# Adaptive-norm Mamba block on one core: decay subtraction and clamp move from VectorE to ScalarE, the convolution goes in pairs of tiles

## The chip, the cores and the metric

The kernel runs on one core of a Trainium2 chip. The metric is the device time of one launch in microseconds; three runs of the kernel before were timed. A profile shows one further look at the same program, instruction by instruction. The engines are TensorE (PE for its matmuls, PEld for its weight loads), VectorE (DVE), ScalarE (ACT), GpSimd (POOL) and SyncE (SP), which issues DMAs.

## The reference, cut to what matters

Two sequences of 2048 tokens and 512 channels go through a norm with shift and scale, a state-space mixer with a gated residual, and then a norm, a feed-forward part with a gated residual. The change touches only the mixer:

```python
zxbcdt = u @ W_in.T                                     # 512 -> 1024 z, 1280 xBC, 16 dt
dt = jax.nn.softplus(dt_raw + dt_bias)                  # 16 heads
xBC = jax.nn.silu(causal_conv(xBC, W_conv, 4 taps) + b_conv)
x, Bm, Cm = split(xBC)                                  # 1024, 128, 128
# per chunk, with cs the running sum of dt*A and decay[l, s] = exp(cs[l] - cs[s]) for s <= l:
Y = ((C B^T) * decay) @ X + (C @ state) * exp(cs)
state = exp(cs_last) * state + B^T (X * exp(cs_last - cs))
y = (Y + Dp * X) * silu(z)
out = (y * rsqrt(mean(y*y) + 1e-5) * norm_w) @ W_out.T
```

## The kernel before, in words

The mixer works in 16 turns of 256 tokens (SC), each of NC = 2 chunks of 128. A turn n projects its own tokens, and does the decay and state work of the turn before it (u = n - 1) beside that; so a 17th turn has only the second half. Turns 0 to 2 and the last are unrolled, the others run in a loop whose body is two turns. There is no scheduler: the order on each engine is written out by hand in the `turn` functions (L572 GpSimd, L709 ScalarE, L983 VectorE, L1210 TensorE, L472 SyncE), and semaphores that count steps tie the engines together. An engine runs strictly in this order, so a wait holds up all behind it.

Around the change, in turn n:

- TensorE (L1210): scores_G, y_off(0,0), project_zdt(0), transpose_x(0), project_zdt(1), transpose_B(0), y_off(0,1), tile 0, y_diag(0,0), tile 1, y_diag(0,1), tiles 2 and 3, states(0,0), tile 4, states(0,1), transpose_x(1), tile 5, transpose_B(1), y_off(1,0), tile 6, cumulate, y_diag(1,0), transpose_g(0), tiles 7 and 8, project_out(0), y_off(1,1), y_diag(1,1), tile 9, z parts 0 and 1 with states(1,0) behind the first and states(1,1) behind the second, transpose_g(1), z parts 2 and 3, transpose_ln for turn n + 1, project_out(1). The pairs in brackets are (chunk, half of the heads).
- The projections alternate between two PSUM banks (`A_ORDER`, L375). A projection waits until the last but one before it has been read out (`a_emptied`): project_zdt(1) of turn n + 1 takes the bank of project_out(1) of turn n, and so waits for ScalarE's scale_out(1) (L702).
- ScalarE (L709) reads out each of the 10 tiles twice (L615, a copy for the convolution's taps; L616, its last tap with the bias), and at the end of the turn does evac_ln (L589), widen (L602), the SiLU of tiles 8 and 9 (L619), exp_sums (L678), four exp_decay (L686) of 128x1024 each, and scale_out(1). SiLU and Exp need a table load each, two in a turn.
- VectorE (L983): conv (L813) adds three taps to a tile, each instruction waiting for the one before it on the same tile. softplus (L843) is a chain of 15 instructions on 128x32. sums (L869) reads cumulate's products from PSUM. diff (L882), 32 instructions of 128x128 in a turn, makes min(cs[l] - cs[s], 0) in place in `A.L`, which a DMA has filled with cs[l] in every partition. read_state (L951) adds a state product from PSUM to the state; states(c,1) on TensorE uses the same PSUM bank and waits until read_state(c,0) is done. y_off(1,0) waits for read_state(0,1).
- GpSimd (L572) multiplies X by D (L535), and gates y in three instructions (L543, L547, L549) once VectorE has read y_diag and y_off of the chunk.
- SyncE (L472) writes the sums out (L484) and loads them back over all partitions (L493).

Of the kernel before, what the change touches and what calls it, by code (L numbers as in the profile page):

```python
# [8 lines left out]
ALU = mybir.AluOpType  # L9
ACT = mybir.ActivationFunctionType  # L10
# [28 lines left out]
def wait(eng, sem, n, per, c):  # L39

    v = count(n, per, c)
    if isinstance(v, int) and v <= 0:
        return
    eng.wait_ge(sem, v)
# [278 lines left out]
def mixer_stage(nc, T, A):  # L323
# [4 lines left out]
    D, DI, H, HD = T.D, T.DI, T.H, T.HD  # L328
    KD, KI = D // P, DI // P
    KH = KI // 2  # L330
    MX = T.CD // P
# [10 lines left out]
    with ExitStack() as ctx:  # L342
# [11 lines left out]
            sem(s) for s in ("silu_done", "siluq_done", "e3_done", "edt_done", "decay_done", "sq_done"))  # L354
        stats_step, normed, split, conv_step, softplus_step, sums_step = (
            sem(s) for s in ("stats_step", "normed", "split", "conv_step", "softplus_step", "sums_step"))
        tail_step, diff_done, G_masked, M_done, Xdec_done = (
            sem(s) for s in ("tail_step", "diff_done", "G_masked", "M_done", "Xdec_done"))
        yoff_read, ydiag_read, S_step = sem("yoff_read"), sem("ydiag_read"), sem("S_step")
        rstd_step, XD_done, y_summed, gated, rs_step, out_step = (  # L360
            sem(s) for s in ("rstd_step", "XD_done", "y_summed", "gated", "rs_step", "out_step"))
# [226 lines left out]
        def _(act):  # L588
# [29 lines left out]

            def silu_tile(n, b, m):  # L619

                wait(act, conv_step, n, 3 * MX, 3 * (m + 1))
                x = A.xc[b][:, m, :]
                nc.scalar.activation(x, x, ACT.Silu).then_inc(silu_done, 1)

# [53 lines left out]
            def exp_sums(u):  # L678
# [4 lines left out]
                wait(act, yoff_read, u, 2 * NC, 0)  # L683
                nc.scalar.activation(A.e3[:], A.s3[:], ACT.Exp).then_inc(e3_done, 1)

            def exp_decay(u, c, f):  # L686
                wait(act, diff_done, u, 2 * NC, 2 * c + f + 1)
                x = A.L[c][:, f * HH:(f + 1) * HH, :]
                nc.scalar.activation(x, x, ACT.Exp).then_inc(decay_done, 1)

            def exp_dt(n):
                wait(act, softplus_step, n, SP_STEPS, 2)
# [16 lines left out]
            def turn(n, b):  # L709
# [57 lines left out]
                if nxt:  # L767
                    evac_ln(after(n), 1 - b, n)
                if own:
                    widen(n, 1)  # L770
                    silu_tile(n, b, 8)
                    silu_tile(n, b, 9)
                    exp_sums(n)
                    exp_decay(n, 0, 0)
                    exp_decay(n, 0, 1)
                    exp_decay(n, 1, 0)
                    exp_decay(n, 1, 1)
# [6 lines left out]
        def _(dve):  # L784
# [25 lines left out]
                nc.vector.tensor_tensor(A.hTlo[:, :, s], h, A.hThi[:, :, s].bitcast(F32),  # L810
                                        ALU.subtract).then_inc(split, 1)

            def conv(n, b, m):  # L813

                a_wait(dve, a_emptied, n, ("m", m), 1)
                for j in range(3):
                    if j:
                        wait(dve, conv_step, n, 3 * MX, 3 * m + j)
                    nc.vector.scalar_tensor_tensor(A.xc[b][:, m, :], A.raw[:, m, j:j + SC], A.wconv[:, m, j:j + 1],  # L819
                                                   A.xc[b][:, m, :], ALU.mult, ALU.add).then_inc(conv_step, 1)  # L820

            def tails(n, b):

# [19 lines left out]
            def softplus(n):  # L843


                wait(dve, edt_done, n, 1, 1)
                step = [2]

                def did(ins):
                    ins.then_inc(softplus_step, 1)  # L850
                    step[0] += 1

                    wait(dve, softplus_step, n, SP_STEPS, step[0])

                did(nc.vector.tensor_scalar(sp2[:], sp1[:], 2.0, None, ALU.add))
                did(nc.vector.reciprocal(sp2[:], sp2[:]))
                did(nc.vector.tensor_tensor(sp3[:], sp1[:], sp2[:], ALU.mult))
                did(nc.vector.tensor_tensor(sp4[:], sp3[:], sp3[:], ALU.mult))
                did(nc.vector.tensor_scalar(sp5[:], sp4[:], 1.0 / 15.0, None, ALU.mult))
                for k in (13, 11, 9, 7, 5, 3):  # L860
                    did(nc.vector.scalar_tensor_tensor(sp5[:], sp5[:], 1.0 / k, sp4[:], ALU.add, ALU.mult))
                did(nc.vector.scalar_tensor_tensor(sp5[:], sp5[:], 1.0, sp3[:], ALU.add, ALU.mult))
                did(nc.vector.tensor_scalar(sp0[:], sp0[:], 0.0, None, ALU.max))
                did(nc.vector.scalar_tensor_tensor(sp5[:], sp5[:], 2.0, sp0[:], ALU.mult, ALU.add))

                nc.vector.tensor_tensor(A.a[:], sp5[:], A.negA[:].unsqueeze(1).broadcast_to([P, NC, H]),
                                        ALU.mult).then_inc(softplus_step, 1)

            def sums(n):  # L869

                wait(dve, cs_done, n, 1, 1)

                wait(dve, e3_done, n, 1, 0)
                wait(dve, cs_out, n, 16, 0)
                wait(dve, diff_done, n, 2 * NC, 0)
                nc.vector.tensor_copy(A.s3[:, 0:2 * NC * H], small[:, 0:2 * NC * H]).then_inc(sums_step, 1)
                wait(dve, sums_step, n, 3, 1)
                nc.vector.tensor_tensor(A.s3[:, 2 * NC * H:3 * NC * H], A.s3[:, NC * H:2 * NC * H],
                                        A.s3[:, 0:NC * H], ALU.subtract).then_inc(sums_step, 1)
                nc.vector.tensor_copy(A.csT[:], small[0:NC * H, 2 * P:3 * P]).then_inc(sums_step, 1)  # L880

            def diff(u, c, f):  # L882

                if f == 0:

                    wait(dve, cs_in[c], u, 16, 16)
                    wait(dve, sums_step, u, 3, 3)
                for h in range(f * HH, (f + 1) * HH):
                    last = nc.vector.tensor_scalar(A.L[c][:, h, :], A.L[c][:, h, :], A.s3[:, c * H + h:c * H + h + 1],
                                                   0.0, ALU.subtract, ALU.min)  # L890
                last.then_inc(diff_done, 1)

            def mask_G(u):
                wait(dve, G_done, u, 1, 1)
# [88 lines left out]
            def turn(n, b):  # L983
                u = before(n)
                own, bef, nxt = has_own(n), has_before(n), has_next(n)
                if bef:
                    mask_G(u)
                    scores(u, 0, 0)
                    read_yoff(n, u, b, 0, 0)
                    scores(u, 0, 1)  # L990
                if own:
                    dt_first(n, b)
                if bef:
                    scores(u, 1, 0)
                    scores(u, 1, 1)
                    read_ydiag(u, 0, 0)
                    read_yoff(n, u, b, 0, 1)
                if own:
                    conv(n, b, 0)
                if bef:  # L1000
                    read_ydiag(u, 0, 1)
                    decay_X(n, u, 0)
                if own:
                    conv(n, b, 1)
                if bef:
                    read_state(u, b, 0, 0)
                if own:
                    conv(n, b, 2)
                if bef:
                    read_state(u, b, 0, 1)  # L1010
                if own:
                    softplus(n)
                    conv(n, b, 3)
                if n == 0:
                    setup.vector_turn0(dve, 0)
                if own:
                    sums(n)
                if bef:
                    low_g(n, u, 0)
                    read_yoff(n, u, b, 1, 0)  # L1020
                if own:
                    conv(n, b, 4)
                    conv(n, b, 5)
                if bef:
                    read_ydiag(u, 1, 0)
                measure(n, 0)
                if nxt:
                    stats(after(n), 0)
                    stats(after(n), 1)
                if own:  # L1030
                    conv(n, b, 6)
                if bef:
                    read_yoff(n, u, b, 1, 1)
                    read_ydiag(u, 1, 1)
                    decay_X(n, u, 1)
                if nxt:
                    norm(after(n), n, 0)
                    norm(after(n), n, 1)
                if own:
                    conv(n, b, 7)  # L1040
                if bef:
                    read_state(u, b, 1, 0)
                if own:
                    conv(n, b, 8)
                if bef:
                    read_state(u, b, 1, 1)
                    low_g(n, u, 1)
                if own:
                    conv(n, b, 9)
                    tails(n, b)  # L1050
                if n == 0:
                    setup.vector_turn0(dve, 1)
                if own:
                    diff(n, 0, 0)
                    diff(n, 0, 1)
                    diff(n, 1, 0)
                    diff(n, 1, 1)
                if nxt:
                    split_h(after(n), n, 0)
                    split_h(after(n), n, 1)  # L1060
                if own:
                    measure(n, 1)
# [637 lines left out]
```

## Time and profile before

| | us |
|---|---|
| three runs | 1736.09, 1740.42, 1739.21 |
| median | 1739.21 |
| span of the profiled execution | 1740.9 |
| mean granted TensorE clock, share of full | 0.938 |

The page gives no time for the profiled execution beside its span, so the span stands for it; it is 1.7 us over the median and 0.5 us over the slowest run. The mixer takes the first two thirds of the span, the feed-forward part, which the change doesn't touch, the rest. In the profile a row of the timeline gives start, length, engine, line, what is written and read, how many instructions were merged into the row, and in brackets the engine's idle time just before it with what ended it.

### The profile page before, as it was taken

The numbers are of one execution on the slowest core, as the hardware profiler recorded it, in microseconds if no ns is written. First come the engines' busy times: TensorE is split into PE (matmuls) and PEld (weight loads), VectorE is DVE, ScalarE is ACT, GpSimd is POOL, SyncE is SP. The second block draws the span as 40 slices with busy tenths as digits, with TensorE's granted clock in tenths as the row PEclk, the third lists the DMA queues.
The fourth block names the chain that finished last, engine by engine and source line by source line (L and its number), as shares of the span: only waits on it lengthen the run. The fifth ranks groups of instructions, "written<-read, shape, count | busy, mean of one in ns | idle before, by whom it ended". The sixth has DMA issues, their size and how long they took to land. (4 is left out here: it accounts for less than half of the span.)

```text
span 1740.9 us, 26906 instructions
## 1 busy us (share of the span) xinstructions
PE 1569.5 (90%) x8289; PEld 1276.2 (73%) x8289; DVE 1248.8 (72%) x2460; ACT 627.0 (36%) x1208; POOL 492.0 (28%) x440
## 2 busy tenths in 40 slices
PE   5989889988988898989988999875899999999998
PEld 5977777767767777767777777753688888888887
DVE  3779998888888988988988889853546445544543
ACT  3345445444554454434544444430211111201200
POOL 1323423433334233433342333433011111111111
PEclk9799999998999999989998999986899999999999
DMA  8312212121121111211221121104320120120110
GB/s 259 126 42 76 98 46 74 68 79 73 61 84 67 42 73 67 79 73 37 87 83 49 73 67 67 74 31 144 146 73 7 67 73 12 60 72 18 54 49 26
DMA packets 61377, 124.25 MB, mean 71 GB/s; under 512 B 13296, under 2 KB 15984, under 8 KB 56816
## 3 DMA queue, kind: packets, MB, share of 16 engines
q1 hardware_dynamic: 55632, 114.68, 18.9%
q10 hardware_dynamic: 5664, 8.65, 1.4%
q8 instruction: 31, 0.51, 0.1%
q14 instruction: 50, 0.41, 0.1%
HBM read 97.62 MB, written 25.69 MB: 71 GB/s over the span
## 5 line engine op out<-in xcount | busy, mean ns | idle before, releaser
L819 DVE SCALAR_TENSOR_TENSOR xBC<-conv_in,wconv,xBC 128x256 f32<-128x256 f32 x480 | 300.0, 629 | 12.7 <-ACT xBC L616 1.3
L1398 ACT ACTIVATE silu_gate<-bank,sgate 128x512 f32<-128x512 f32 x88 | 60.7, 689 | 383.4 <-PE bank L1517 383.4
L1183 PE MATMUL bank<-X,B_rows 128*128 128x512 f32 x128 | 90.8, 799 | 92.9 <-DVE state L955 88.7
L1452 DVE SCALAR_TENSOR_TENSOR hidden<-bank,sup,silu_gate 128x512 f32<-128x512 f32 x88 | 66.0, 750 | 145.8 <-PE bank L1517 145.8
L615 ACT ACTIVATE conv_in<-bank 128x256 f32<-128x256 f32 x160 | 61.5, 385 | 255.6 <-PE bank L1086 255.6
L1171 PEld LDWEIGHTS bank<-X,decay 128*128 128x128 f32 x1024 | 123.6, 195 | 30.8 <-issue 23.7
L1517 PE MATMUL bank<-ff_h_high,W_gate 128*128 128x512 f32 x352 | 141.5, 402 | 2.4 <-DVE ff_h_low L1440 2.4
L1171 PE MATMUL bank<-X,decay 128*128 128x64 f32 x1024 | 127.0, 278 | 16.4 <-DVE X_D L948 16.4
L1517 PE MATMUL bank<-ff_h_low,W_gate 128*128 128x512 f32 x352 | 140.1, 398 | 0.0
L1549 PE MATMUL bank<-W_down,hidden_high 128*128 128x512 f32 x352 | 139.5, 396 | 0.0
L1549 PE MATMUL bank<-W_down,hidden_low 128*128 128x512 f32 x352 | 139.5, 396 | 0.0
L1517 PE MATMUL bank<-ff_h_high,W_up 128*128 128x512 f32 x352 | 139.3, 396 | 0.0
L1517 PE MATMUL bank<-ff_h_low,W_up 128*128 128x512 f32 x352 | 139.0, 395 | 0.0
L543 POOL TENSOR_TENSOR y<-y,X_D 128x1024 f32<-128x1024 f32 x32 | 105.6, 3300 | 113.6 <-DVE X_D L948 113.6
L1086 PE MATMUL bank<-h_high,W_in_high 128*128 128x256 f32 x640 | 134.4, 335 | 0.0
L1379 POOL TENSOR_TENSOR ff_x_resid<-ff_branch,ff_x_resid 128x512 f32<-128x512 f32 x32 | 41.3, 1291 | 317.1 <-DVE ff_branch L1494 317.1
L564 POOL TENSOR_TENSOR branch<-branch,gate_row 128x512 f32<-128x512 f32 x32 | 41.5, 1298 | 285.3 <-ACT branch L707 285.3
L1207 PE MATMUL bank<-W_out,gT 128*128 128x512 f32 x256 | 115.0, 592 | 0.0
L1086 PEld LDWEIGHTS bank<-h_high,W_in_high 128*128 128x128 f32 x640 | 97.3, 204 | 21.7 <-issue 21.7
L1086 PE MATMUL bank<-W_in_high,h_high 128*128 128x272 f32 (+2 forms) x384 | 97.7, 379 | 14.1 <-DVE W_in_low L211 13.3
L1086 PE MATMUL bank<-h_low,W_in_high 128*128 128x256 f32 x640 | 106.5, 290 | 0.0
L1086 PE MATMUL bank<-h_high,W_in_low 128*128 128x256 f32 x640 | 103.1, 283 | 0.0
(170 smaller groups left out, 3493.2 us busy)
## 6 DMA issues: line engine op xcount, KB each, us to landing
decay<-sums_scratch SPq DMA_DIRECT2D x32, 1024.0 KB, 4.7
wq_rows<-wqT SPq DMA_DIRECT2D x33, 256.0 KB, 4.0
widened_scratch<-wq_rows SPq DMA_DIRECT2D x33, 256.0 KB, 2.0
x_tile<-x SPq DMA_DIRECT2D x32, 256.0 KB, 2.8
x_resid<-x SPq DMA_DIRECT2D x32, 256.0 KB, 2.7
x_scratch<-x_resid SPq DMA_DIRECT2D x32, 256.0 KB, 2.0
ff_x_tile<-x_scratch SPq DMA_DIRECT2D x32, 256.0 KB, 3.6
ff_x_resid<-x_scratch SPq DMA_DIRECT2D x32, 256.0 KB, 4.0
```

The costliest lines, as they stand in the source:

```text
L543: nc.gpsimd.tensor_tensor(A.yt[:], A.yt[:], A.XD[:], ALU.add).then_inc(y_summed, 1)
L564: nc.gpsimd.tensor_tensor(A.ob[:], A.ob[:], T.gate_row[1 - b][:], ALU.mult).then_inc(out_step, 1)
L615: nc.scalar.activation(A.raw[:, m, 3:3 + SC], ps[:, 0:SC], ACT.Copy)
L819: nc.vector.scalar_tensor_tensor(A.xc[b][:, m, :], A.raw[:, m, j:j + SC], A.wconv[:, m, j:j + 1], A.xc[b][:, m, :], ALU.mult, ALU.add).the ...
L1086: mm = nc.tensor.matmul(out, lhs(wp, ap), rhs(wp, ap), start=(i == 0), stop=(i == last))
L1171: mm = nc.tensor.matmul(ydiag[:, h * HD:(h + 1) * HD], A.L[c][:, g, :], A.X[:, g * HD:(g + 1) * HD], start=True, stop=True)
L1183: nc.tensor.matmul(state[:, 0:W], A.Btok[:], A.X[:, f * W:(f + 1) * W], start=True, stop=True).then_inc(state_done, 1)
L1207: mm = nc.tensor.matmul(ps[:], A.gT[:, k, :], A.Wo[:, k, :], start=False, stop=(k == KI - KH - 1))
L1398: nc.scalar.activation(B.sg[m % 2][:], gates[m % 2][:], ACT.Silu, scale=T.sgate[:, m:m + 1]) \
L1452: nc.vector.scalar_tensor_tensor(B.hid[m % 2][:], ups[m % 2][:], T.sup[:, m:m + 1], B.sg[m % 2][:], ALU.mult, ALU.mult).then_inc(hid_step, 1)
L1517: mm = nc.tensor.matmul(ps[:], W[:, k, m * P:(m + 1) * P].bitcast(dt), h[:, k, :].bitcast(dt), start=(k == 0 and a == 0), stop=(k == KD - ...
L1549: mm = nc.tensor.matmul(downs[c % 2][:], h[:, m, s].bitcast(dt), B.Wd[:, m, :].bitcast(dt), start=(m == 0 and a == 0), stop=(m == KH - 1 a ...
```

## The change

Five edits:

1. VectorE's diff is gone. ScalarE gets falls (16 instructions per chunk), which makes max(cs[s] - cs[l], 0) by Relu with the bias from `A.s3` and a scale of -1; exp_decay then takes a scale of -1. falls(0) stands between evac_ln and widen, falls(1) between exp_sums and exp_decay.
2. conv becomes conv_pair: six instructions that alternate between two tiles. It waits until both are read out.
3. softplus becomes a generator; one step of it is issued behind each instruction of pairs 1 and 2, and the rest behind pair 2.
4. The places of the convolution in VectorE's turn move: tiles 0 to 9 were done one or two at a time between the other steps.
5. In the second half of the turn read_state(1,0) comes ahead of the two norms, behind pair 4.

silu_tile waits for the counts that fit the new order.

```diff
+            def falls(u, c):
+
+                wait(act, cs_in[c], u, 16, 16)
+                wait(act, sums_step, u, 3, 3)
+                for h in range(H):
+                    x = A.L[c][:, h, :]
+                    last = nc.scalar.activation(x, x, ACT.Relu, bias=A.s3[:, c * H + h:c * H + h + 1], scale=-1.0)
+                last.then_inc(fall_done, 1)
+
             def exp_decay(u, c, f):
-                wait(act, diff_done, u, 2 * NC, 2 * c + f + 1)
+                wait(act, fall_done, u, NC, c + 1)
                 x = A.L[c][:, f * HH:(f + 1) * HH, :]
-                nc.scalar.activation(x, x, ACT.Exp).then_inc(decay_done, 1)
+                nc.scalar.activation(x, x, ACT.Exp, scale=-1.0).then_inc(decay_done, 1)
...
                 if own:
+                    falls(n, 0)
                     widen(n, 1)
                     silu_tile(n, b, 8)
                     silu_tile(n, b, 9)
                     exp_sums(n)
+                    falls(n, 1)
                     exp_decay(n, 0, 0)
...
+            def conv_pair(n, b, p, between=None):
+
+                a_wait(dve, a_emptied, n, ("m", 2 * p + 1), 1)
                 for j in range(3):
...
+                    for m in (2 * p, 2 * p + 1):
+                        if j:
+                            wait(dve, conv_step, n, 3 * MX, 6 * p + 2 * j + m % 2 - 1)
+                        nc.vector.scalar_tensor_tensor(A.xc[b][:, m, :], A.raw[:, m, j:j + SC],
+                                                       A.wconv[:, m, j:j + 1], A.xc[b][:, m, :], ALU.mult, ALU.add) \
+                            .then_inc(conv_step, 1)
+                        if between:
+                            between()
...
-                if own:
-                    conv(n, b, 0)
                 if bef:
                     read_ydiag(u, 0, 1)
                     decay_X(n, u, 0)
                 if own:
-                    conv(n, b, 1)
+                    conv_pair(n, b, 0)
                 if bef:
                     read_state(u, b, 0, 0)
                 if own:
-                    conv(n, b, 2)
+                    steps = softplus(n)
+                    conv_pair(n, b, 1, lambda: next(steps))
                 if bef:
                     read_state(u, b, 0, 1)
                 if own:
-                    softplus(n)
-                    conv(n, b, 3)
+                    conv_pair(n, b, 2, lambda: next(steps))
+                    for _ in steps:
+                        pass
...
                 if own:
-                    conv(n, b, 6)
+                    conv_pair(n, b, 3)
                 if bef:
                     read_yoff(n, u, b, 1, 1)
                     read_ydiag(u, 1, 1)
                     decay_X(n, u, 1)
+                if own:
+                    conv_pair(n, b, 4)
+                if bef:
+                    read_state(u, b, 1, 0)
                 if nxt:
                     norm(after(n), n, 0)
                     norm(after(n), n, 1)
...
                 if n == 0:
                     setup.vector_turn0(dve, 1)
-                if own:
-                    diff(n, 0, 0)
-                    diff(n, 0, 1)
-                    diff(n, 1, 0)
-                    diff(n, 1, 1)
                 if nxt:
                     split_h(after(n), n, 0)
```

## Rows read from the trace of the kernel before

**Rows 1.** The page: the span; busy time, share of it and instructions by engine.

```profile
span 1740.9 us, 26906 instructions
PE 1569.5 (90%) x8289; PEld 1276.2 (73%) x8289; DVE 1248.8 (72%) x2460; ACT 627.0 (36%) x1208; POOL 492.0 (28%) x440
```

**Rows 2.** Busy time by stretch: two turns, a wait of TensorE, the stretch behind it.

```profile
core 0: us, PE busy (x) PEld busy (x) DVE busy (x) ACT busy (x) POOL busy (x), PEclk, DMA share, GB/s
582.36:722.30 139.94, 124.98 (x729) 101.28 (x728) 121.00 (x248) 65.91 (x135) 50.67 (x40) 0.94 0.19 68
600.50:603.60 3.10, 0.00 (x0) 0.00 (x0) 3.06 (x4) 0.84 (x2) 2.17 (x2) 1.00 0.00 0
603.60:608.50 4.90, 4.89 (x23) 4.12 (x24) 4.36 (x16) 1.19 (x2) 0.00 (x0) 0.65 0.00 0
```

**Rows 3.** Waits: who waited for whom, us in total, times, longest.

```profile
PE bank L1183 <- DVE state L955: 88.7, 32, 3.2
```

**Rows 4.** Groups of instructions: the moved subtraction, and two read-outs of a tile.

```profile
L889 DVE TENSOR_SCALAR decay<-decay,sums 128x128 f32<-128x128 f32 x512 | 101.7, 279 | 0.1
L616 ACT ACTIVATE xBC<-bank,bconv,wconv 128x256 f32<-128x256 f32 x160 | 89.7, 561 | 0.0
L615 ACT ACTIVATE conv_in<-bank 128x256 f32<-128x256 f32 x160 | 61.5, 385 | 255.6 <-PE bank L1086 255.6
```

**Rows 5.** Timeline of ScalarE: the end of one turn, then one read-out later.

```profile
575.18 1.94 ACT L598 ACTIVATE X_D<-bank,modc 128x256 f32<-128x256 f32 x4
576.99 0.64 ACT L605 ACTIVATE wq_rows<-wq_rows 128x512 f32<-128x512 int32 x1
...
578.26 1.28 ACT L684 ACT_TABLE_LOAD   x1
579.55 0.28 ACT L684 ACTIVATE exp_sums<-sums 128x96 f32<-128x96 f32 x1
579.74 3.88 ACT L689 ACTIVATE decay<-decay 128x1024 f32<-128x1024 f32 x4
583.53 0.67 ACT L707 ACTIVATE branch<-bank,inv_rms 128x512 f32<-128x512 f32 x1
...
608.97 0.56 ACT L616 ACTIVATE xBC<-bank,bconv,wconv 128x256 f32<-128x256 f32 x1
```

**Rows 6.** Timeline of TensorE in one turn: project_zdt(1), states(0,1), y_diag(1,0), y_off(1,1), states(1,1).

```profile
585.24 0.75 PE L1086 MATMUL bank<-W_in_high,h_high 128*128 128x272 f32 x4
...
603.61 1.41 PE L1183 MATMUL bank<-X,B_rows 128*128 128x512 f32 x2 [3.11 <-DVE state L955]
...
611.66 2.00 PE L1171 MATMUL bank<-X,decay 128*128 128x64 f32 x16
...
623.44 1.02 PE L1161 MATMUL bank<-state,xBC 128*128 128x512 f32 x2
...
635.61 2.08 PE L1183 MATMUL bank<-X,B_rows 128*128 128x512 f32 x2 [2.89 <-DVE state L955]
```

**Rows 7.** Timeline of VectorE in the same turn, and one row of the next.

```profile
597.52 5.43 DVE L819 SCALAR_TENSOR_TENSOR xBC<-conv_in,wconv,xBC 128x256 f32<-128x256 f32 x3
602.88 0.68 DVE L955 TENSOR_TENSOR state<-bank,state 128x512 f32<-128x512 f32 x1
603.48 1.51 DVE L819 SCALAR_TENSOR_TENSOR xBC<-conv_in,wconv,xBC 128x256 f32<-128x256 f32 x3
...
606.93 1.32 DVE L861 SCALAR_TENSOR_TENSOR softplus<-softplus 128x32 f32<-128x32 f32 x6
...
616.67 2.96 DVE L819 SCALAR_TENSOR_TENSOR xBC<-conv_in,wconv,xBC 128x256 f32<-128x256 f32 x6
...
654.13 0.42 DVE L897 TENSOR_TENSOR G_masked<-bank,triu 128x256 f32<-128x256 f32 x1 [3.01 <-issue]
```

**Rows 8.** Timeline of GpSimd: the first instruction of the gate.

```profile
596.62 3.22 POOL L543 TENSOR_TENSOR y<-y,X_D 128x1024 f32<-128x1024 f32 x1 [6.52 <-DVE X_D L948]
```

More of the change, by code:

```diff
@@ L356, in mixer_stage @@
             sem(s) for s in ("stats_step", "normed", "split", "conv_step", "softplus_step", "sums_step"))
-        tail_step, diff_done, G_masked, M_done, Xdec_done = (
-            sem(s) for s in ("tail_step", "diff_done", "G_masked", "M_done", "Xdec_done"))
+        tail_step, fall_done, G_masked, M_done, Xdec_done = (
+            sem(s) for s in ("tail_step", "fall_done", "G_masked", "M_done", "Xdec_done"))
         yoff_read, ydiag_read, S_step = sem("yoff_read"), sem("ydiag_read"), sem("S_step")
@@ L619, in silu_tile @@
             def silu_tile(n, b, m):
-                wait(act, conv_step, n, 3 * MX, 3 * (m + 1))
+                wait(act, conv_step, n, 3 * MX, 3 * (m + 1) + 2 * (1 - m % 2))
                 x = A.xc[b][:, m, :]
@@ L811, in split_h @@
                                         ALU.subtract).then_inc(split, 1)
-            def conv(n, b, m):
-                a_wait(dve, a_emptied, n, ("m", m), 1)
+            def conv_pair(n, b, p, between=None):
+                a_wait(dve, a_emptied, n, ("m", 2 * p + 1), 1)
                 for j in range(3):
[L817 to L820, printed above, removed]
+                    for m in (2 * p, 2 * p + 1):
[6 more added lines that the diff above has]
+                            between()
             def tails(n, b):
@@ L846, in softplus @@
                 wait(dve, edt_done, n, 1, 1)
[L847 to L864, printed above, removed]
+                nc.vector.tensor_scalar(sp2[:], sp1[:], 2.0, None, ALU.add).then_inc(softplus_step, 1)
@@ new lines, in softplus @@
+                yield
+                wait(dve, softplus_step, n, SP_STEPS, 3)
+                nc.vector.reciprocal(sp2[:], sp2[:]).then_inc(softplus_step, 1)
+                yield
+                wait(dve, softplus_step, n, SP_STEPS, 4)
+                nc.vector.tensor_tensor(sp3[:], sp1[:], sp2[:], ALU.mult).then_inc(softplus_step, 1)
+                yield
+                wait(dve, softplus_step, n, SP_STEPS, 5)
+                nc.vector.tensor_tensor(sp4[:], sp3[:], sp3[:], ALU.mult).then_inc(softplus_step, 1)
@@ new lines, in softplus @@
+                yield
+                wait(dve, softplus_step, n, SP_STEPS, 6)
+                nc.vector.tensor_scalar(sp5[:], sp4[:], 1.0 / 15.0, None, ALU.mult).then_inc(softplus_step, 1)
+                yield
+                for i, k in enumerate((13, 11, 9, 7, 5, 3)):
+                    wait(dve, softplus_step, n, SP_STEPS, 7 + i)
+                    nc.vector.scalar_tensor_tensor(sp5[:], sp5[:], 1.0 / k, sp4[:], ALU.add, ALU.mult) \
+                        .then_inc(softplus_step, 1)
+                    yield
@@ new lines, in softplus @@
+                wait(dve, softplus_step, n, SP_STEPS, 13)
+                nc.vector.scalar_tensor_tensor(sp5[:], sp5[:], 1.0, sp3[:], ALU.add, ALU.mult) \
+                    .then_inc(softplus_step, 1)
+                nc.vector.tensor_scalar(sp0[:], sp0[:], 0.0, None, ALU.max).then_inc(softplus_step, 1)
+                yield
+                wait(dve, softplus_step, n, SP_STEPS, 15)
+                nc.vector.scalar_tensor_tensor(sp5[:], sp5[:], 2.0, sp0[:], ALU.mult, ALU.add) \
+                    .then_inc(softplus_step, 1)
@@ L866, in softplus @@
+                yield
+                wait(dve, softplus_step, n, SP_STEPS, 16)
                 nc.vector.tensor_tensor(A.a[:], sp5[:], A.negA[:].unsqueeze(1).broadcast_to([P, NC, H]),
                                         ALU.mult).then_inc(softplus_step, 1)
+                yield
             def sums(n):
@@ L874, in sums @@
                 wait(dve, cs_out, n, 16, 0)
-                wait(dve, diff_done, n, 2 * NC, 0)
+                wait(dve, fall_done, n, NC, 0)
                 nc.vector.tensor_copy(A.s3[:, 0:2 * NC * H], small[:, 0:2 * NC * H]).then_inc(sums_step, 1)
@@ L880, in sums @@
                 nc.vector.tensor_copy(A.csT[:], small[0:NC * H, 2 * P:3 * P]).then_inc(sums_step, 1)
[L882 to L891, printed above, removed]
             def mask_G(u):
@@ L1020, in turn @@
                     read_yoff(n, u, b, 1, 0)
-                if own:
-                    conv(n, b, 4)
-                    conv(n, b, 5)
                 if bef:
@@ L1038, in turn @@
                     norm(after(n), n, 1)
[L1039 to L1044, printed above, removed]
                 if bef:
@@ L1048, in turn @@
                 if own:
-                    conv(n, b, 9)
                     tails(n, b)
@@ L1052, in turn @@
                     setup.vector_turn0(dve, 1)
-                if own:
-                    diff(n, 0, 0)
-                    diff(n, 0, 1)
-                    diff(n, 1, 0)
-                    diff(n, 1, 1)
                 if nxt:
```

## The prediction
> **What bounds the kernel now.** The shares of the page come first: VectorE is busy 72% of the span and ScalarE 36% [rows 1], which invites moving work from one to the other. But the feed-forward third dilutes both, so I read two turns of the mixer alone: in 139.94 us, 69.97 a turn, TensorE works 124.98, VectorE 121.00, ScalarE 65.91 [rows 2]. TensorE and VectorE are both nearly full, and what matters is who waits for whom. TensorE's large wait is the one for VectorE's read of a state product, 88.7 us in 32 cases, two in each turn [rows 3]; the clock behind such a wait is granted at 0.65 over 4.90 us [rows 2], between the levels of 1.2 and 2.4 GHz, so each also costs up to 0.35 x 4.9 = 1.7 us of slow matmuls.
>
> Why is VectorE late there? Three convolution instructions take 5.43 us where the same three take 1.51 a little later [rows 7]. In the long case GpSimd is in its gate, whose first instruction alone lasts 3.22 us [rows 8]. So the wait is a local chain: second half of y_diag, read_ydiag, decay_X, three convolutions held up by the gate, read_state, TensorE. Less work on VectorE elsewhere doesn't shorten it.
>
> The timelines give one turn as a chain of TensorE's. I count from the end of evac_ln on ScalarE, E = 575.18 + 1.94 = 577.1 [rows 5]. Then project_zdt(1) starts at E + 8.1, states(0,1) 18.4 later, y_diag(1,0) 8.05 later, y_off(1,1) 11.8 later, states(1,1) 12.2 later [rows 6], and about 10 us on the next E. At zdt(1) ScalarE is just ahead: scale_out(1), which frees the bank, ends at 583.53 + 0.67 = 584.20, 1.0 us before [rows 5, 6].
>
> **Falls on ScalarE.** The trace shows no Relu and no 128x128 activation from SBUF, so I bound its price. An Exp of 128x96 takes 0.28 us and the next instruction starts 0.19 after it; a 1024-column Exp takes (3.88 + 3 x 0.09) / 4 = 1.04 [rows 5]. The slope is (1.04 - 0.28) / 928 = 0.82 ns a column, so 128 columns take 0.31 long and 0.22 start to start. L616 has two per-partition operands more than L615 and takes 561 - 385 = 176 ns more at the same shape [rows 4]; one operand, the bias, is 0.09. I take 0.31 us start to start: 4.9 a chunk, 9.8 a turn. Bounds: VectorE's own 101.7 / 512 = 0.20 below [rows 4], 0.40, no overlap at all, above.
>
> The Trainium skill prices this too (ScalarE: Activation LUTs, What ACT_TABLE_LOAD costs): an ACTIVATE with a pointer bias takes 280 ns + 0.833 ns a column, and neighbours overlap by 93 ns. That would make 0.294 each, 9.4 a turn; the trace's own rows are within 5% of it. The same page (Rules for kernel authors) says to use VectorE, not ScalarE, for relu, max, min and add: it speaks against this edit, as the row of L889 does.
>
> All of it lies in one line: evac_ln, falls(0), widen, SiLUs, table load, exp_sums, falls(1), four exp_decay, scale_out(1). Before, that ran 7.1 us from E [rows 5]; it becomes 16.9. ScalarE's spare time, which makes the 36%, lies elsewhere in the turn. Queued behind scale_out(1) are evac_zdt and evac_x, and project_zdt(1) on TensorE waits for scale_out(1) itself. It had 1.0 us of slack, so it goes from E + 8.1 to E + 16.9: **+8.8 us a turn**. VectorE's scores wait for exp_decay in the same stretch, so what diff freed there (101.7 / 16 = 6.4 us) becomes idle time. Nothing of the diff's removal is on TensorE's path in a first turn of a pair; in the other, VectorE loses 3.01 us at the loop's edge [rows 7], and that now falls into the wait: -3.0 every second turn.
>
> **States(0,1).** read_state(0,0) comes behind six convolutions, not three. Within a tile, three take 1.51 us, 0.52 from start to start; six in two tiles take 2.96 [rows 7], so a start that depends on nothing is 0.41 after the last. Three held up by the gate as before, three more at 0.41: +1.2. conv(0) no longer stands ahead of read_ydiag(0,1): -0.4 (TensorE's product arrives only then; the bound is 0 to -0.8). The clock behind a new wait of some 7 us at zdt(1): 0 to +1.7, I take half, since VectorE's scores run beside it. Sum +1.6.
>
> **Softplus and cumulate.** Its steps cost 0.22 each as a chain [rows 7] and, set between convolutions, some 0.11 (length less overlap); the work shrinks by 1.4 us. But pair 2 waits for the read-out of tile 5, which ends at 608.97 + 0.56 = 609.5, 5.9 after states(0,1) [rows 5, 6]; conv(3) and softplus waited for no such thing. From there six convolutions and six steps, 6 x 0.52 = 3.1, two last steps 0.4, and cumulate's products 0.8 give y_diag(1,0) at 10.2 behind states(0,1), where it was 8.05: +2.1. So the interleaving saves VectorE time and makes the dependent product later.
>
> **The rest.** Pair 3 costs 2.5 for 1.5, ahead of y_off(1,1), which VectorE now waits for anyway: 0. read_state(1,0) sits behind pair 4, again held up by the gate, instead of behind two norms and conv(7), all held up by it too: three instructions behind three of GpSimd's, then 1.2: +0.2. The norms come behind it, with about 10 us until the next E: 0. SyncE: its loads of `A.L` land long before falls asks for them, and its stores follow the turn: 0. The other convolutions lie under TensorE's work, which would cover 3 us more.
>
> **Sum.** 8.8 + 1.6 + 2.1 + 0.2 = 12.7 in a first turn, 9.7 in the other, 11.2 in the mean. Between the first and the last of the 16 turns (512 / 32 [rows 4]) lie 14 such steps: 157. The first boundary has no scale_out, but evac_zdt stands behind the same queue: 10. After the last own turn there is no evac_ln to wait for, and a part is hidden: 7. Span 1740.9 + 174 = 1915, and by the 1.7 us that the profiled execution lies over the median, **1913**.
>
> **Rivals.**
> - *The local waits go.* If GpSimd's gate doesn't hold up a pair, both state waits vanish: 88.7 / 16 = 5.5 a turn, with two slow stretches of 1.7, and 1.5 of the loop's edge, 10.4. Against 8.7 at the boundary that is -1.7 a turn, 26 in all: 1713, faster. It decides where TensorE's wait before states(0,1) falls under 1 us. For it: pairs are shorter. Against: L819 at 5.43 [rows 7]. Chance 0.09.
> - *A cheap fall.* At 0.20 each the chain shrinks by 32 x 0.11 = 3.5 a turn, 53 in all: 1860. Chance 0.15.
> - *It cancels.* With a cheap fall the boundary costs 8.8 - 3.5 = 5.3 a turn, and the 5.5 of state waits goes as in the first rival: about 1740. Chance 0.03.
> - *More slow clock.* TensorE now has four waits of over 2 us in a turn; if each of the two new ones costs a full slow stretch, that is 3.4 - 0.85 more, 38 in all, and with 0.33 a fall 1960. Chance 0.13.
> - *Relu wants a table of its own.* Then falls(0) and falls(1) bring some four loads of 1.28 us [rows 5], 5.1 a turn: 1990. Against: there are Identity and Copy between the SiLUs with no load. Chance 0.02. The Trainium skill (ScalarE: Activation LUTs, Table sets) has relu in every set, so no load by it.
> - The change does what it says: no case that it doesn't.
>
> The forecast has 0.58. **Range** 1845 to 1962: the lower end is the cheap fall with half of cumulate's 2.1 a turn gone (1860 - 15), the upper the slow clock. Within 0.3%, 5 us, this kernel can't be told from no change. Faster 0.09, same 0.03, slower 0.88.
>
> **What would show it.** Right: ScalarE's 512 new instructions at 0.37 to 0.42 us, 0.31 apart; project_zdt(1) idle for some 7 us, ended by ScalarE's scale_out; a new wait of 2 us on cumulate for VectorE's last softplus step; states(0,1) waiting 4 us; the mixer's turn at 81 us; VectorE's busy time down by over 100 us. Wrong: a turn under 70 us, or TensorE at zdt(1) without a wait, which would mean that the chain from evac_ln to scale_out is not serial or not on the path.

## The result, and the profile after

The changed kernel takes 1989.36 us (median of 4, 1988.98 to 1993.22) against 1737.65 us: 1.145 times as long (1.142 to 1.148). Slower, as forecast, but by 252 us where the forecast had 174, and beyond the range's 1962.

The page after: VectorE has lost 157 us of work, ScalarE has gained 147, and the span is 246 longer [rows 1].

```profile
span 1987.3 us, 26810 instructions
PE 1657.5 (83%) x8289; PEld 1347.9 (68%) x8289; DVE 1091.4 (55%) x1948; ACT 773.6 (39%) x1720; POOL 474.4 (24%) x440
```

TensorE does the same 8289 matmuls in 88 us more of busy time; that is the first sign of a slower clock. These are TensorE's large waits after, with one of VectorE's. Of the four of TensorE, before had only the one of states(c,1) [rows 3]; its scores_G waited in all 2.7 us:

```profile
PE bank L1187 <- DVE state L970: 105.7, 32, 4.0
...
PE bank L1090 <- ACT branch L716: 92.7, 14, 6.7
...
DVE decay L921 <- ACT decay L698: 83.6, 16, 6.1
...
PE bank L1139 <- DVE dtA L891: 37.2, 16, 3.2
...
PE bank L1129 <- ACT xBC L623: 24.5, 15, 7.4
```

L716 is scale_out, L1090 behind it project_zdt(1), L1139 cumulate. L1129 is scores_G, which waits some 1.2 us a turn for the SiLU of tiles 8 and 9, now behind falls(0); the prediction doesn't name this wait, but it ends before project_zdt(1) waits for the same chain, so it adds nothing. ScalarE's timeline at a turn's end shows the chain, to be set beside [rows 5]: 16 falls, widen, SiLUs, table load, exp_sums, 16 falls, four exp_decay, scale_out.

```profile
691.50 1.93 ACT L598 ACTIVATE X_D<-bank,modc 128x256 f32<-128x256 f32 x4
693.32 4.79 ACT L692 ACTIVATE decay<-decay,sums 128x128 f32<-128x128 f32 x16
697.99 0.63 ACT L605 ACTIVATE wq_rows<-wq_rows 128x512 f32<-128x512 int32 x1
...
700.54 0.28 ACT L684 ACTIVATE exp_sums<-sums 128x96 f32<-128x96 f32 x1
700.73 4.77 ACT L692 ACTIVATE decay<-decay,sums 128x128 f32<-128x128 f32 x16
705.41 3.88 ACT L698 ACTIVATE decay<-decay 128x1024 f32<-128x1024 f32 x4
709.19 0.67 ACT L716 ACTIVATE branch<-bank,inv_rms 128x512 f32<-128x512 f32 x1
```

And TensorE in that turn, the marks of [rows 6] plus cumulate (740.61) and y_diag(1,0) (741.50):

```profile
709.91 1.27 PE L1090 MATMUL bank<-W_in_high,h_high 128*128 128x272 f32 x4 [6.61 <-ACT branch L716]
...
730.23 2.08 PE L1187 MATMUL bank<-X,B_rows 128*128 128x512 f32 x2 [3.91 <-DVE state L970]
...
740.61 0.41 PE L1139 MATMUL bank<-dtA,triu 128*128 128x32 f32 x2 [2.28 <-DVE dtA L891]
...
741.50 3.37 PE L1175 MATMUL bank<-X,decay 128*128 128x64 f32 x16
...
756.46 1.02 PE L1165 MATMUL bank<-state,xBC 128*128 128x512 f32 x2
...
768.74 1.69 PE L1187 MATMUL bank<-X,B_rows 128*128 128x512 f32 x2 [3.00 <-DVE state L970]
```

E, the end of evac_ln as in the prediction, is 691.50 + 1.93 = 693.43, and the next one is at 779.02. The turn divides so:

| step, us | before | forecast | after |
|---|---|---|---|
| E to project_zdt(1) | 8.1 | 16.9 | 16.5 |
| to states(0,1) | 18.4 | 20.0 | 20.3 |
| to y_diag(1,0) | 8.05 | 10.2 | 11.3 |
| to y_off(1,1) | 11.8 | 11.8 | **15.0** |
| to states(1,1) | 12.2 | 12.4 | 12.3 |
| to the next E | 10.0 | 10.0 | 10.3 |
| turn | 68.5 | 81.2 | 85.6 |

In this turn, 3.2 us of the 4.4 that the forecast lacks stand in one line, where no instruction changed and nothing waits. The turns aren't all alike: over 15 of them, from the timelines, this line takes 15.0 us in nine and 13.4 in six, 14.3 in the mean, where before it takes 11.8 in all. The line above it takes 11.1 in the mean, and before 6.4 to 9.2, 8.1 in the mean. The next rows are busy time by stretch, with the granted clock in the third column from the end. In the changed kernel they show what lies behind the wait before states(0,1), then the stretch with the wait before cumulate, then the 14.90 us from y_diag(1,0) to y_off(1,1):

```profile
730.23:735.90 5.67, 5.67 (x24) 4.53 (x25) 3.56 (x13) 1.20 (x2) 0.00 (x0) 0.58 0.00 0
735.90:740.50 4.60, 2.43 (x16) 1.74 (x14) 3.56 (x15) 2.88 (x7) 0.10 (x1) 1.00 0.00 0
741.50:756.40 14.90, 14.90 (x69) 12.53 (x69) 8.16 (x18) 6.23 (x12) 3.20 (x5) 0.77 0.24 89
```

The last piece is in the kernel before

```profile
611.66:623.44 11.78, 11.78 (x69) 9.34 (x69) 8.62 (x20) 7.40 (x15) 3.37 (x6) 1.00 0.31 113
```

The same 69 matmuls take 11.78 us at the full 2.4 GHz, and 14.9 where the granted clock was 0.77 in the mean, so in part at 1.2 GHz: 0.23 x 14.9 = 3.4 us.

### The profile page after: what moved, and what is told of

It reads as the page before. It is cut to its first block and busy times, and to the rows that moved or that the text cites. A ratio compares the mean times of both kernels' runs of the same rounds, so it can differ in the third digit from the quotient of the medians.

```text
span 1987.3 us, 26810 instructions
## 1 busy us (share of the span) xinstructions
PE 1657.5 (83%) x8289; PEld 1347.9 (68%) x8289; DVE 1091.4 (55%) x1948; ACT 773.6 (39%) x1720; POOL 474.4 (24%) x440
## 5 line engine op out<-in xcount | busy, mean ns | idle before, releaser
L831 DVE SCALAR_TENSOR_TENSOR xBC<-conv_in,wconv,xBC 128x256 f32<-128x256 f32 x480 | 331.4, 730 | 59.5 <-ACT xBC L616 57.7
L1090 PE MATMUL bank<-W_in_high,h_high 128*128 128x272 f32 (+2 forms) x384 | 110.1, 417 | 106.7 <-ACT branch L716 92.7
L1090 PEld LDWEIGHTS bank<-W_in_high,h_high 128*128 128x128 f32 x384 | 74.7, 233 | 131.3 <-ACT branch L716 96.0
L692 ACT ACTIVATE decay<-decay,sums 128x128 f32<-128x128 f32 x512 | 152.8, 394 | 0.0
L1175 PEld LDWEIGHTS bank<-X,decay 128*128 128x128 f32 x1024 | 139.2, 216 | 13.9 <-issue 13.8
L1090 PE MATMUL bank<-h_high,W_in_high 128*128 128x256 f32 x640 | 146.6, 357 | 0.0
L1175 PE MATMUL bank<-X,decay 128*128 128x64 f32 x1024 | 142.0, 299 | 1.3 <-DVE X_D L963 1.3
L1090 PEld LDWEIGHTS bank<-h_high,W_in_high 128*128 128x128 f32 x640 | 107.7, 225 | 28.5 <-issue 21.3
L921 DVE TENSOR_TENSOR decay<-decay,G_masked 128x1024 f32<-128x1024 f32 x64 | 78.8, 1253 | 83.6 <-ACT decay L698 83.6
```

Of the source, the lines that this page charges most:

```text
L692: last = nc.scalar.activation(x, x, ACT.Relu, bias=A.s3[:, c * H + h:c * H + h + 1], scale=-1.0)
L921: nc.vector.tensor_tensor(x, x, A.Gm[:, c, :].unsqueeze(1).broadcast_to([P, HH, P]), ALU.mult) \
L1090: mm = nc.tensor.matmul(out, lhs(wp, ap), rhs(wp, ap), start=(i == 0), stop=(i == last))
L1175: mm = nc.tensor.matmul(ydiag[:, h * HD:(h + 1) * HD], A.L[c][:, g, :], A.X[:, g * HD:(g + 1) * HD], start=True, stop=True)
```

## The experiments

Each run was timed beside the kernel before, on the same chip. Ratios are to that kernel.

### Each half alone

`e1_falls_only` is the kernel before with edit 1 alone:

```diff
                 if own:
+                    falls(n, 0)
                     widen(n, 1)
...
                     exp_sums(n)
+                    falls(n, 1)
...
-                    diff(n, 0, 0)
-                    diff(n, 0, 1)
-                    diff(n, 1, 0)
-                    diff(n, 1, 1)
```

> The kernel before with edit 1 alone: the falls on ScalarE at the places the change gives them, the convolution and softplus as before. Theory: the chain from evac_ln to scale_out(1) grows by 16 x 0.30 x 2 = 9.6 us, and project_zdt(1) starts 8.35 us later in every turn (E + 16.5, not E + 8.1); less 1.5 a turn that VectorE lost at the loop's edge, plus 1 to 2 of slow clock behind the new wait: +8 to +9 a turn over 15 boundaries, 1865 us (1840 to 1890). Rival, the new order on VectorE is what costs and ScalarE's chain hides: under 1780 us.

Measured: 1858.1 us, 1.072 (1.069 to 1.074), as expected. ScalarE's longer chain costs by itself, and the wait at its end is the one of the change:

```profile
650.63 1.27 PE L1081 MATMUL bank<-W_in_high,h_high 128*128 128x272 f32 x4 [6.61 <-ACT branch L716]
```

`e2_pairs_only` is the changed kernel with diff back on VectorE at its old place, and no falls.

> The changed kernel with the subtraction and clamp back on VectorE at their old place: pairs, interleaved softplus and the new order stay. Theory: the wait on cumulate for the last softplus step (2.3 us) with the slow clock behind it (2 to 4 us) and 0.8 to 1.2 us of a longer wait before states(0,1) remain, the wait on project_zdt(1) goes: +4 to +7 a turn, 1820 us (1790 to 1850). Rival, the order is the main cost: over 1880 us. Rival, only the falls cost: under 1760 us.

Measured: 1841.16 us, 1.062 (1.060 to 1.064), inside the expected range. The wait on project_zdt(1) is gone and cumulate's is untouched:

```profile
662.88 0.40 PE L1144 MATMUL bank<-dtA,triu 128*128 128x32 f32 x2 [2.28 <-DVE dtA L880]
```

Alone, the two halves cost 7.2% and 6.2%, 13.4% in sum, and together 14.5%: neither hides the other.

### What in the pairs costs

`e3_softplus_ahead` is the changed kernel with the later softplus steps taken out of pair 2:

```diff
-                    conv_pair(n, b, 2, lambda: next(steps))
                     for _ in steps:
                         pass
+                    conv_pair(n, b, 2)
```

> The changed kernel with one edit: the softplus steps that were set into pair 2 run ahead of pair 2, so that they no longer stand behind the read-out of tile 5. They end some 5.6 us after states(0,1) starts and TensorE comes to cumulate at 7 to 8. Theory (the wait brings a stretch of slow clock with it): 2.3 us of wait and 3 to 4 of slow matmuls go in each turn, 1989 - 15 x 5.7 = 1904 us (1890 to 1925). Rival (the slow clock there comes from the earlier waits and stays): 1989 - 15 x 2.3 = 1954 us.

Measured: 1885.58 us, 1.087 (1.085 to 1.090): 5.8% of the time of before comes off the changed kernel's 14.5%. That is nearly all that the pairs cost in e2 (6.2%), and more than my theory's 85 us: 1885.58 lies just under the expected range. What held the softplus up in the changed kernel is VectorE's wait for the read-out of tile 5:

```profile
736.86 0.48 DVE L831 SCALAR_TENSOR_TENSOR xBC<-conv_in,wconv,xBC 128x256 f32<-128x256 f32 x1 [3.06 <-ACT xBC L616]
```

In e3 the timeline of TensorE has no wait at cumulate, and what follows runs as before: 8.04 us from states(0,1) (682.70) to y_diag(1,0), 11.77 from there to y_off(1,1).

```profile
682.70 1.19 PE L1187 MATMUL bank<-X,B_rows 128*128 128x512 f32 x2 [3.91 <-DVE state L970]
...
690.74 2.00 PE L1175 MATMUL bank<-X,decay 128*128 128x64 f32 x16
...
702.51 1.02 PE L1165 MATMUL bank<-state,xBC 128*128 128x512 f32 x2
```

Against the table: 3.2 us less in each of these two steps, 6.4 for a wait of 2.28 us. Over 15 turns the two steps together are 4.1 to 6.6 us shorter than in the changed kernel, 5.6 in the mean. Of the 3.2 in the first step, 0.9 lies ahead of the wait: the stretch behind states(0,1) is slower in that turn (its two matmuls take 2.08 us, here 1.19, after the same wait of 3.91). In other turns of the changed kernel they take 1.12, and the second step is then the one of 13.4 us. What sets which turn gets which isn't shown.

### Is it the idle time that lowers the clock?

`e8_filled_wait` is the changed kernel with TensorE kept busy in that wait; the products go to columns that nothing reads:

```diff
-                wait(pe, softplus_step, n, SP_STEPS, SP_STEPS)
-
                 wait(pe, G_masked, n, 1, 0)
+                for _ in range(10):
+                    nc.tensor.matmul(small[:, 3 * P:4 * P], A.triu[:], A.ones[:], start=True, stop=True)
+                wait(pe, softplus_step, n, SP_STEPS, SP_STEPS)
```

> The changed kernel with ten matmuls of 128x128 on constants, into columns of the bank that nothing reads, ahead of cumulate's wait for the last softplus step: the wait of 2.3 us stays as long but TensorE works through it. Theory (the 3.2 us that y_diag(1,0) to y_off(1,1) takes longer is slow clock brought on by that idle time): 1989 - 15 x 3 = 1944 us (1925 to 1960), the granted clock of that stretch back at 1.0. Rival (that stretch is slow for another reason, or the fill comes late): 1980 to 2010 us.

Measured: 1938.5 us, 1.117 (1.114 to 1.119), as expected: 51 us less than the changed kernel, with no instruction taken away and 320 matmul records (20 in each of 16 turns) added. TensorE's timeline, and the granted clock behind it:

```profile
713.33 2.40 PE L1136 MATMUL bank<-ones,triu 128*128 128x128 f32 x20
715.69 0.41 PE L1140 MATMUL bank<-dtA,triu 128*128 128x32 f32 x2
```

```profile
716.58:728.36 11.78, 11.78 (x70) 9.34 (x69) 8.33 (x18) 6.12 (x12) 3.28 (x5) 1.00 0.31 114
```

11.78 us, to the hundredth what it was before the change, and 11.77 to 11.80 in all 15 turns. The data come as late as in the change: cumulate starts 9.6 to 10.5 us behind states(0,1), and there 9.6 to 10.7. So the idle time brings the slow stretch behind it.

`e10_before_filled` asks the same of the kernel before, at its two waits before states(c,1):

```diff
                 if f:
+                    for _ in range(13):
+                        nc.tensor.matmul(small[:, 3 * P:4 * P], A.triu[:], A.ones[:], start=True, stop=True)
                     wait(pe, S_step, u, 4 * NC, 4 * c + 3)
```

> The kernel before with thirteen matmuls of 128x128 on constants, into columns that nothing reads, ahead of each wait before states(c,1): TensorE works through some 2.9 us of the 3.0 us that it waits, and nothing comes earlier. Theory (a wait of 3 us costs its length and then a stretch of slow clock worth 1.5 to 2 us): the slow stretches go, 3 us a turn, 1738 - 45 = 1693 us (1680 to 1710). Rival (the slow matmuls behind a wait lie beside VectorE's work and cost nothing, or the clock falls in any case): 1730 to 1750 us.

Measured: 1689.47 us, 0.976 (0.971 to 0.980), as expected: 43 us gained by matmuls whose products nobody reads. The stretches behind the two waits are at full clock, where [rows 2] had 0.65 behind the first:

```profile
647.45:653.80 6.35, 6.35 (x43) 5.17 (x43) 5.73 (x22) 2.62 (x7) 0.00 (x0) 1.00 0.00 0
677.90:684.00 6.10, 6.08 (x35) 5.03 (x36) 5.58 (x18) 2.10 (x4) 0.21 (x1) 1.00 0.01 4
```

From states(0,1) to y_diag(1,0) it now takes 6.4 us in all 15 turns, and before 8.1 in the mean. So the slow stretch behind that wait was worth 1.7 us in the mean, the price that the prediction gave it, and up to 2.8 in single turns.

### Is it ScalarE's work or its place?

`e6_falls_spread` is the kernel before with all 512 falls on ScalarE, in pieces, in its idle slots:

```diff
+                    falls(n, 0, 0, 6)
                 if bef:
                     scale_out(n, u, 0)
...
+                    falls(n, 0, 6, 14)
                     evac_tile(n, b, 9)
                     silu_tile(n, b, 5)
+                    falls(n, 0, 14, 16)
...
+                if own:
+                    falls(n, 1, 0, 8)
+                if bef:
                     evac_g(n, u, 1)
...
                     exp_sums(n)
+                    falls(n, 1, 8, 16)
```

> The kernel before with all 512 falls on ScalarE, as in e1_falls_only, but at other places: those of chunk 0 in ScalarE's idle slots before scale_out(0), evac_tile(9) and silu_z(0), the first eight of chunk 1 before evac_g(1), the last eight behind exp_sums. The work is the same, only 2.4 us of it is left between evac_ln and scale_out(1). Theory (the place costs, not the work): project_zdt(1) comes at E + 9.5, the turn is back at 69 to 71 us, 1735 us (1715 to 1755). Rival (ScalarE's load as such, or two engines at the same buffers): it stays within 30 us of the 1858 us of e1_falls_only.

Measured: 1754.88 us, 1.011 (1.009 to 1.013), at the upper end of the expected range. With the same instructions, 103 us of e1's loss are gone: the place costs, not the work. Of the 18 us that stay, most is what was left in the chain, a wait of up to 1.1 us at project_zdt(1):

```profile
PE bank L1087 <- ACT branch L717: 15.3, 14, 1.1
```

So ScalarE had the room, and a freer VectorE still brought no gain: TensorE's waits before states(c,1) are the old ones (91.6 us in all).

### The local waits, and a kernel that beats both

`e4_states_early` moves two steps of the kernel before, and has nothing of the change:

```diff
                     decay_X(n, u, 0)
+                    read_state(u, b, 0, 0)
                 if own:
                     conv(n, b, 1)
-                if bef:
-                    read_state(u, b, 0, 0)
...
                     decay_X(n, u, 1)
+                    read_state(u, b, 1, 0)
                 if nxt:
                     norm(after(n), n, 0)
                     norm(after(n), n, 1)
                 if own:
                     conv(n, b, 7)
-                if bef:
-                    read_state(u, b, 1, 0)
```

> The kernel before with two moves and nothing of the change: read_state(c,0) comes directly behind decay_X(c), ahead of the convolution and norms that GpSimd's gate holds up. Theory (the waits before states(c,1) are a local chain through the gate): both waits of 3.0 us and the slow clock behind them go, part of it given back because VectorE has 60.5 us of work in a turn of 70: 1650 us (1610 to 1695). Rival (VectorE's total work sets the turn): 1725 to 1745 us.

Measured: 1686.88 us, 0.973 (0.971 to 0.975), inside the expected range. Both waits before states(c,1) are gone; TensorE does the two products 2.3 us apart and without a pause.

```profile
644.84 1.02 PE L1181 MATMUL bank<-X,B_rows 128*128 128x512 f32 x2
...
647.12 1.02 PE L1181 MATMUL bank<-X,B_rows 128*128 128x512 f32 x2
```

That is 47 us, less than the 88 of my middle: TensorE now meets VectorE at other places, before y_off (22.3 and 20.4 us in all), project_zdt (14.3) and cumulate (13.5). These waits are short, but not free of slow clock: behind 1.5 us before y_off(1,0) and 0.9 before cumulate, y_diag(1,0) to y_off(1,1) takes 13.4 or 14.9 us in eight of 15 turns, and 11.8 in the others.

`e5_states_early_split` adds e6's idea, three quarters of the falls in ScalarE's slots and diff(1,1) left on VectorE.

> e4_states_early with three quarters of the falls on ScalarE in idle slots (chunk 0, and half of chunk 1 between the two read-outs of evac_g(1)) and the last quarter left to VectorE. Theory (in e4 VectorE's subtraction at the turn's end holds up split_h and the scores, and TensorE waits 1.0 and 0.4 to 3.2 us for them): 2 to 3 us a turn go, 1650 us (1635 to 1670). Rival (the bound in e4 is TensorE's own work and the loop): 1680 to 1690 us.

Measured: 1662.13 us, 0.957 (0.956 to 0.959), as expected. VectorE was the one waited for at the turn's end: of TensorE's waits in e4, the 14.3 us at project_zdt and the 20.4 at y_off are gone. Here, moving this work off VectorE pays.

`e7_split_interleaved` takes tiles 1 and 2, 4 and 5, 7 and 8 of that kernel in turn.

> e5_states_early_split with tiles 1 and 2, 4 and 5, 7 and 8 taken in turn, instruction by instruction, at places where they already stood together, so that no pair waits for a read-out that a single tile didn't. VectorE gets 3 x 0.5 us a turn back. Theory (interleaving as such is right, its place in the change was wrong): 0 to -1 us a turn against e5, 1645 us. Rival (it costs, as the read-out of the later tile is waited for): over e5 by 10 us or more.

Measured: 1658.4 us, 0.955 (0.953 to 0.957), not the 1645 that I expected. The medians are 4 us apart and the interval overlaps e5's, so a gain from interleaving by itself isn't shown; the cost of 10 us or more that the rival had is not there.

`e9_softplus_first` reorders the middle of e7:

```diff
-                    conv_two(n, b, 1)
+                    conv(n, b, 1)
                 if bef:
                     read_state(u, b, 0, 1)
                 if own:
                     softplus(n)
-                    conv(n, b, 3)
+                    conv_two(n, b, 2)
```

> e7_split_interleaved with the middle of the turn in another order: tile 1, read_state(0,1), softplus as one block, then tiles 2 and 3 in turn. TensorE waits in e7 1.2 us before y_off(1,0) for read_state(0,1) and 0.9 before cumulate for softplus, in most turns. Theory: both go, 1.5 to 2.5 us a turn, 1630 us (1620 to 1645). Rival (TensorE's own work is the bound by now, or the wait moves to the scores): 1650 to 1660 us.

Measured: 1647.98 us, 0.953 (0.948 to 0.957): above the expected range and nearer to the rival. The median is 10 us under e7's where 28 were expected, and the intervals of the two ratios overlap, so even this gain isn't clear of the noise. The wait before y_off(1,0) is gone, the one on cumulate stays, as does one on the first read_ydiag:

```profile
PE bank L1191 <- DVE X_D L978: 21.4, 15, 5.1
...
PE bank L1155 <- DVE dtA L897: 12.8, 14, 1.1
```

It has the lowest median of all, 5% under the kernel before and 17% under the changed one. Its state reads come from e4 and its split from e5; what filled waits would add to it was not tried.

## Why the prediction was wrong in size

- **What bounds the kernel**: right. TensorE's chain and local waits set the turn, and VectorE's total didn't: e6 frees VectorE of 6.4 us a turn and gains nothing, e4 takes away the two waits before states(c,1) and gains 2.7%.
- **Falls on ScalarE, +8.8 a turn**: right, 8.35. A fall lasts 394 ns and starts (4.79 - 0.39) / 15 = 0.293 us after the last; I had 0.40 and 0.31. The Trainium skill's price (ScalarE: Activation LUTs, What ACT_TABLE_LOAD costs) was 0.387 and 0.294, nearer than my rows.
- **States(0,1), +1.6**: right, 1.95, the wait is 3.91 instead of 3.11.
- **Softplus and cumulate, +2.1**: this is the step that failed. The mechanism was right, and pair 2 starts late for tile 5 as it said, but the term was mis-sized: cumulate's wait was forecast as a delay and nothing more. In the turn of the table it measured 3.2 up to y_diag(1,0) and 3.2 again up to y_off(1,1), where "the rest" put 0; over 15 turns 3.0 and 2.6 in the mean. e3 removes both with the wait, e8 removes the second while the wait stays. The second alone, 2.6 in each of some 15 turns, is about half of the 72 us that the span lies over the forecast.
- **"More slow clock", 38 us in all, 0.13**: the right rival with the wrong price. I took 1.7 us for a slow stretch from the one window of 4.90 us at 0.65 [rows 2], charged the new wait at project_zdt(1) half of it and cumulate's nothing. For the wait before states(0,1) the price holds in the mean (e10). Behind cumulate's wait the slow stretch is worth 3.2 us in nine turns and 1.6 in six, and e8 prices it at 51 us over the mixer. Why this wait, shorter than the one before states(0,1), is followed by more is open. A second wait close behind another could be the cause, but no run here separates that.
- **The sum over turns**: a first turn grew by 17.1 us where I had 12.7, and from 784.94 to 869.32, the starts of scores_G, the next took 84.4, where before it was 139.94 - 68.5 = 71.4: 13.0 for my 9.7. The credit for the loop's edge was right: the turns of the changed kernel take 84.4, 85.6 or 86.0 us in an order that doesn't follow the loop's two. The slow clock is missing from both terms. From the first states(0,1) to the last, 14 steps, a turn grew by 15.8 in the mean, 221 us where I had 157; the two ends grew by 25 where I had 17.
- The other rivals fell: no table load came with Relu (16 loads each for SiLU and Exp in the turns, as before), a fall wasn't cheap, and GpSimd's gate held up the pairs (six convolutions in 6.63 us).

## What to carry to other kernels

Before moving work to an engine that a page shows idle, find the instructions in line behind the new place and who waits for the last of them: the same 512 instructions cost 7% at the turn's end and 1% in the slots. When a dependent chain is interleaved with other work, ask what that other work waits for; softplus was done with fewer gaps and later. And price a new wait of TensorE twice, by its length and by the matmuls behind it: here taking away 2.3 us of idle time gave back 4.1 to 6.6 us a turn.

## What the runs showed of the hardware

- Behind a wait of 2.28 us the granted clock was 0.77 in the mean over 14.9 us in which TensorE worked without a pause, so 1.2 GHz for part of them. Ten matmuls on constants in the wait kept it at 1.00 and gave back 2.6% of the changed kernel's time (e8). In the kernel before, 26 in a turn gave 2.4% (e10), about as much as removing both state waits (e4: 2.7%). In e4 even waits of 1.5 and 0.9 us were followed by slow stretches in about half of the turns.
- VectorE's convolution, which reads SBUF twice, waits for GpSimd's instruction to end. In the changed kernel the gate's three instructions end at 725.26, 727.24 and 728.11, and the first three of these six convolutions each end within 0.5 us behind one of them; six that meet no gate take 2.46 us (754.80).

```profile
722.94 6.63 DVE L831 SCALAR_TENSOR_TENSOR xBC<-conv_in,wconv,xBC 128x256 f32<-128x256 f32 x6
```

- An addition that reads PSUM once and SBUF once wasn't held up: e4's read_state runs from 646.00 to 646.69, across the gate's first instruction (643.10 to 646.32) and second (from 646.48), and takes its usual 0.69 us.
